# Channel heads of a four-layer kernel: scores and transposed scores issued in bursts of four row groups at both ends of the pipeline

## The reference

```python
# _L3_xattn_ref(q, k, v, gamma), called with (_layernorm(x), ctx, ctx, gamma); h = 8, dq = dv = 16
qh = q.reshape(B, h, dq, Lq)
kh = k.reshape(B, h, dq, Lk)
vh = v.reshape(B, h, dv, Lk)
qk = jnp.einsum('bhdq,bhdl->bhql', qh, kh) * scale
sm = jax.nn.softmax(qk, axis=-1)
ret = jnp.einsum('bhql,bhdl->bhdq', sm, vh)
return gamma * ret.reshape(B, Dv, Lq)
```

## Time and profile before

| | |
|---|---|
| median of 3 runs | 1308.56 us (1308.42 to 1309.82) |
| profiled execution | 1305.17 us, of which the span is 1303.0 us |
| PE busy | 1089.4 us (84%), mean granted clock 0.918 |
| DVE, ACT, POOL busy | 766.5, 494.2, 577.3 us |
| channel heads | about 861 to 1091 us of the span |
| their lead-in (scores alone) | about 873.7 to 887 us |
| their tail (keys alone) | from about 1045 us |
| mixture behind them | from 1091.6 us, its routed tiles from 1130.5 us |

### The profile page before, as it was taken

How to read it: one execution, slowest core, us unless ns; L and a number is a source line. 1 busy time by engine, 2 the same in 40 slices (tenths; PEclk the granted TensorE clock), 3 DMA queues, 4 the chain that set the end, 5 groups by cost and what they waited for, 6 DMA issues and landing times. The chain is left out here.

```text
span 1303.0 us, 25544 instructions
## 1 busy us (share of the span) xinstructions
PE 1089.4 (84%) x7222; PEld 799.5 (61%) x7223; DVE 766.5 (59%) x2814; ACT 494.2 (38%) x1309; POOL 577.3 (44%) x910
## 2 busy tenths in 40 slices
PE   4568799999999983999997999958887795799970
PEld 4355688877777761566655766634554554688860
DVE  6767443244444444687754655457888846555547
ACT  0046221223333320566563234414665532244430
POOL 5550027713333343555561524444333566455550
PEclk9998699999999995899998999977998966899995
DMA  9788962213333327111010234340000622366648
GB/s 399 212 259 280 340 218 108 107 57 110 106 106 106 106 86 314 50 52 64 2 38 22 98 87 134 122 157 1 2 2 2 242 82 84 114 164 164 164 120 320
DMA packets 92301, 169.45 MB, mean 130 GB/s; under 512 B 11102, under 2 KB 70750, under 8 KB 91230
## 3 DMA queue, kind: packets, MB, share of 16 engines
q1 hardware_dynamic: 72393, 107.63, 27.1%
q0 software_dynamic: 17664, 48.91, 10.4%
q10 hardware_dynamic: 2160, 11.86, 2.2%
HBM read 82.75 MB, written 85.61 MB: 129 GB/s over the span
## 5 line engine op out<-in xcount | busy, mean ns | idle before, releaser
L2177 PE MATMUL bank<-weights,xT 128*128 x832 | 240.8, 412 | 0.2 <-ACT xT L2271 0.2
L1999 POOL DMA_INDIRECT slots_out<-weights,y_rows x128 | 122.8, 959 | 134.8 <-DVE y_rows L2443 89.6
L2177 PEld LDWEIGHTS bank<-weights,xT 128*128 128x128 f32 x832 | 142.5, 191 | 24.6 <-issue 0.7
L1993 POOL DMA_INDIRECT slots_in<-xn_wide,row_in x106 | 102.4, 966 | 101.3 <-DMA slots_in<-xs_wide 49.8
L1999 POOL DMA_INDIRECT slots_out<-pack,y_rows x80 | 76.7, 959 | 142.8 <-DVE y_rows L2443 135.3
L2271 ACT COPY xT<-bank 128x256 f32<-128x256 f32 x208 | 77.4, 372 | 116.9 <-PE bank L2169 116.5
L1412 PE MATMUL bank<-ctx,weights 32*128 32x256 f32 x512 | 79.6, 451 | 33.0 <-DVE weights L1566 26.9
L2088 PE MATMUL bank<-xT,weights 128*128 128x256 f32 x416 | 104.5, 396 | 2.3 <-ACT xT L2235 2.3
L1485 ACT ACTIVATE weights<-bank 128x512 f32<-128x512 f32 x128 | 72.6, 596 | 72.0 <-PE bank L1420 72.0
L2420 DVE TENSOR_TENSOR weights<-weights,bank 128x128 f32<-128x128 f32 x128 | 36.8, 288 | 102.4 <-ACT weights L2275 102.4
L1566 DVE TENSOR_REDUCE weights<-bank 128x2 f32<-128x512 f32 x128 | 85.6, 681 | 10.3 <-PE bank L1412 9.8
(11 more groups left out here) (428 smaller groups left out, 2456.4 us busy)
## 6 DMA issues: line engine op xcount, KB each, us to landing
slots_in<-xs_wide SPq DMA_DIRECT2D x16, 2112.0 KB, 19.0
weights<-slots_in SPq DMA_DIRECT2D x96, 132.0 KB, 2.3
xs_wide<-slots_in SPq DMA_DIRECT2D x72, 132.0 KB, 2.3
weights<-slots_out SPq DMA_DIRECT2D x17, 512.0 KB, 11.5
rows<-slots_out SPq DMA_DIRECT2D x16, 512.0 KB, 3.3
weights<-in_l_gu SPq DMA_DIRECT2D x1, 7040.0 KB
pack<-slots_in SPq DMA_DIRECT2D x40, 132.0 KB, 2.1
weights<-in_l_gu ACTq DMA_DIRECT2D x1, 4608.0 KB, 14.4
```

The source lines that it names most:

```text
L1993: pool.indirect_dma_start(out=slots_in, in_=xn_wide[:, t, :], in_offset=None, out_offset=bass.IndirectOffsetOnAxis(ap=row_in[:, t, i:i + 1 ...
L1999: pool.indirect_dma_start(out=slots_out, in_=y[:, n % U, :], in_offset=None, out_offset=bass.IndirectOffsetOnAxis(ap=y_rows[:, n % U:n % U ...
L2177: last = nc.tensor.matmul(out, xT[:, n.c % 2, c, :], flat(gu_w[:, ds(e, 1), c, :]), start=(c == 0), stop=(c == C - 1 and layer != 2))
```

## The change

Scores and keys are no longer always issued two at a time.

- Lead-in: scores 0 to 3, 4 to 7 and 8 to 11 go out in bursts of four, at t = -14, -10 and -6; t = -12, -8 and -4 issue none. From t = -2 on it is as before.
- Tail: keys 116 to 119, 120 to 123 and 124 to 127 go out in bursts of four at t = 116, 120 and 124; t = 118, 122 and 126 issue none. These twelve keys rotate over the six banks 0 to 5 instead of three (`key_bank`); `key_owner` gives the item whose exponential must be done before. Key 116 also waits for all peaks.
- The waits for `b_added` before the lead-in's bursts are for 4, 6 and 8 at t = -14, -10, -6.
- Step 15 issues 24 scatters instead of 28, and the mixture 12 late ones instead of 8.

```diff
-            scatter_in = {13: 6, 14: 6, 15: 28}
+            scatter_in = {13: 6, 14: 6, 15: 24}
...
+            LAST_FOURS = N * NB - 12
+
             def score_bank(s):
                 return bank[s % LEAD] if s < AHEAD else S[s % SB]
+
+            def key_bank(k):
+                return ST[k % TB] if k < LAST_FOURS else bank[k % LEAD]
+
+            def key_owner(k):
+
+                if k < LAST_FOURS:
+                    return k - TB
+                if k - LEAD >= LAST_FOURS:
+                    return k - LEAD
+                return max(m for m in range(LAST_FOURS) if m % TB == k % TB) if k % LEAD >= SB else None
+
+            def scores_at(t):
+                first = t + AHEAD
+                if t < -2:
+                    return range(first, first + 4) if first % 4 == 0 else ()
+                return range(first, min(first + 2, N * NB))
+
+            def keys_at(t):
+                if t >= LAST_FOURS:
+                    return range(t, min(t + 4, N * NB)) if t % 4 == 0 else ()
+                return range(max(t, 0), max(t + 2, 0))
...
-                    queries = [divmod(s, N) for s in (t + AHEAD, t + AHEAD + 1) if s < N * NB]
-                    keys = [divmod(k, N) for k in (t, t + 1) if 0 <= k < N * NB]
+                    queries = [divmod(s, N) for s in scores_at(t)]
+                    keys = [divmod(k, N) for k in keys_at(t)]
...
-                        if N * b + n >= TB:
-                            pe.wait_ge(e_ready, N * b + n - TB + 1)
+                        if N * b + n == LAST_FOURS:
+                            pe.wait_ge(m_ready, N * NB)
+                        owner = key_owner(N * b + n)
+                        if owner is not None and owner >= 0:
+                            pe.wait_ge(e_ready, owner + 1)
...
-                            last = nc.tensor.matmul(ST[(N * b + n) % TB][:, j * L:(j + 1) * L],
+                            last = nc.tensor.matmul(key_bank(N * b + n)[:, j * L:(j + 1) * L],
...
-                    if t < 8 - AHEAD:
-                        pe.wait_ge(b_added, t + AHEAD + 2)
+                    if t in (-14, -10, -6):
+                        pe.wait_ge(b_added, {-14: 4, -10: 6, -6: 8}[t])
...
-                        nc.scalar.activation(eT[:, n].rearrange("p j q -> p (j q)"), ST[t % TB][:], ACT.Exp,
+                        nc.scalar.activation(eT[:, n].rearrange("p j q -> p (j q)"), key_bank(t)[:], ACT.Exp,
...
-            mixture(3, rt, carve, LAST, scattered, 8)
+            mixture(3, rt, carve, LAST, scattered, 12)
```

## The result

| | before | after |
|---|---|---|
| median | 1308.49 us (1307.88 to 1309.82, 4 runs) | 1295.93 us (1294.64 to 1296.95, 4 runs) |
| ratio of the medians | | 0.9902, 95% interval 0.9885 to 0.9919 |
| profiled execution | 1305.17 us, span 1303.0 | 1296.95 us, span 1294.9 |
| the same pair again, in a later series | 1308.15 us (11 runs) | 1297.07 us (6 runs), ratio 0.9914 (0.9899 to 0.9930) |

The kernel is 12.6 us faster in the first series and 11.1 us in the later one; 1299.7 was forecast, that is 8.9 us.

The account below looks back on a forecast made before the run. The prediction took POOL's scatters, held up by the channel heads' tail on half-clock PE, as the bound. Tail -10.4, block's end +0.5 and lead-in +1.0 gave -8.9 us: 1308.56 to 1299.7 us, range 1296.3 to 1305.0.

Parts of the forecast that it names:

- The clock in the tail: Channel heads' tail: PE's granted clock rises from half to full 3 to 5.5 us after t = 116 starts.
- rival A: Tail: the clock stays at one half to the end, gain only 3.0 us, 1305.6 us; chance 0.15.
- Rival C: Tail: bursts of four don't run abreast, each takes 4 us, tail gains 0, 1310.1 us; chance 0.03.
- rival B: Lead-in: bursts with gaps keep the clock low in the batches behind; slower, 1310.5 us; chance 0.04.
- PE's chain and ACT's behind it: Tail: at full clock ACT's row sets values(15,1), starting 12.4 us after t = 116 instead of 23.57.
- The cap: POOL's first sixteen scatters of step 15 let at most 10.9 us of the tail's gain through; 10.4 taken.
- The block's end, +0.5: POOL's ninth scatter after the hole now waits for the block's end: 0.5 us cost, bounds 0 and 1.0.
- The lead-in, +1.0: Lead-in: two DVE stalls of 0.7 us, partly absorbed, plus 0.2 for the clock: +1.0 us, bounds 0 and 2.3.
- the sum, -10.4 + 0.5 + 1.0 = -8.9: Whole kernel: tail, block's end and lead-in terms added, giving a median of 1299.7 us; chance 0.67.
- case D: Lead-in and block's end cost nothing: 1298.2 us, or 1297.7 with the full cap; chance 0.11.
- The profiled execution: Whole kernel's profiled time: 1305.17 - 8.9 = 1296.3 us, its 3.4 us under the median carried over.

Follow-up runs that it names:

- the last experiment: Tail's fours, lead-in in pairs, two scatters moved to step 12, with 22 scatters in step 15 and 12 late instead of 26 and 8: 1298.39 us, 0.9929.
- the lead-in alone: Kernel before with only the lead-in's bursts of four; tail in pairs, 28 scatters in step 15, 8 late: 1308.28 us, ratio 1.0002.
- before, 2nd: Kernel before, unchanged, run and profiled again in a later series: 1307.58 us, ratio 0.9992.
- all four kernels: On the slower chip, against before (1438.29 us): before again 1438.74, tail alone 1434.15, lead-in alone 1436.52, before with filler products 1439.02 us.
- The tail's part: Kernel before with only the tail's bursts of four; lead-in in pairs, 28 scatters in step 15, 8 late: 1296.66 us, ratio 0.9910.

## Why the prediction was right, and where it was off

**The clock in the tail, right.** The full clock was expected 3 to 5.5 us behind the start of t = 116 and came after 2.65 us, a little sooner than that. The row of transposes right behind the first burst did no harm. The rule cited from the Trainium skill (TensorE: Matmul & The Clock Gate, Part 4: PE-mode transpose) would have made this rival A, 1305.6 us; the rows of after refute that outcome here. They don't show what a transpose counts for by itself. Rival C is out by the first burst of sixteen records, 2.09 us where it wanted 4, and rival B by the lead-in's clock, which rose sooner and not later (below).

**PE's chain and ACT's behind it, right within 1 us.** The last values were forecast 12.4 us after t = 116 and came after 11.5.

**The cap, right, and taken too low.** The prediction set 10.9 us as the most that POOL's sixteen scatters let through, and took 10.4. The slots came 1.4 us before the seventeenth scatter began, so the cap was reached in full: from the start of t = 116 to the last scatter it is 76.1 us before and 65.15 after, 10.9 us less. 0.5 us mis-sized.

**The block's end, +0.5, measured 0.** The step named DVE's entry into the mixture as the bound for the ninth scatter. The bound exists (1.1 us in the last experiment), but it moved with the tail: once the hole had closed, the block's work was done before POOL got there. The ninth scatter started 11.5 us behind the last slot instruction (1082.60 less 1071.09), DVE's entry came after 10.9 (1081.95). The error was to compare the ninth scatter with the block's end, both at their old distance from L1808 (the ninth at 10.39 us behind it, the bound at 10.9). With the cap taken as binding, the same working would have had POOL at its own pace there, and not at L1808's.

**The lead-in, +1.0, measured 0 to 0.3.** The stalls came as drawn, two of 0.64 us, and the first subtraction of peaks 0.92 us later. But it doesn't last: 0.3 us were left at t = 116. What fits this is the granted clock, which rose for the batches behind after 21.3 us from the first score (876.00 to 897.3) instead of 24.85 (873.75 to 898.6), and in the lead-in alone after 21.5. For the clock the prediction had added 0.2 us of loss; by this reading it gave some 0.6 back, and no run separates it from other slack.

**The step that failed: the sum, -10.4 + 0.5 + 1.0 = -8.9.** Its mechanism held, but all three terms were mis-sized to the same side. The largest miss is the lead-in's +1.0, which measured 0 to 0.3; the block's end, +0.5, measured 0; the tail's -10.4 measured -10.9. With the measured sizes the sum is -10.6 to -10.9, and from the first score to the end the traces give 10.4 to 10.9. That is case D with the full cap, which the prediction put at 1297.7; the later series has 1297.07. This accounts for 1.7 to 2.0 us of the miss of 3.8 us (1299.7 to 1295.93).

The rest is no term of the change that a trace shows. It lies between some 10.9 us in the stage and a difference of medians of four runs each, 12.6 us with an interval from 10.6 to 15.0; the later series, with 11.1 us (9.2 to 13.2), agrees with the stage. What part of the first 12.6 is chance can't be said more closely. The prediction's range had no term for it: its lower end lay 1.4 us below case D with the full cap, and the first median 0.4 us below that end.

**The profiled execution: near, by luck.** 1296.3 us was forecast and 1296.95 measured. The change gave more than the sum said, and this execution reached the channel heads 2.25 us later than the one of before (876.00 against 873.75); the two largely cancel. The 3.4 us by which the profiled execution of before lay under its median were carried over as if they belonged to the kernel; the one of after lay 1.0 us above its own median. This didn't move the forecast of the median, which is 1308.56 - 8.9 with or without it, but such offsets are why the two whole profiled executions, 8.2 us apart, don't measure the change.

Most of the 3.4 us can be seen to arise long ahead of the change. The windows of a stretch of low clock in before, and in before, 2nd, whose own time is 1308.6 us, 1.0 above its median:

```profile
130.00:151.00 21.00, 13.98 (x59) 12.50 (x60) 9.32 (x38) 5.27 (x12) 2.55 (x5) 0.51 1.09 341
151.00:158.00 7.00, 6.02 (x35) 5.00 (x34) 3.12 (x18) 1.40 (x4) 0.00 (x0) 1.00 1.09 341
```

```profile
130.00:151.00 21.00, 14.13 (x59) 12.65 (x60) 9.16 (x38) 5.27 (x12) 2.56 (x5) 0.51 1.09 341
151.00:158.00 7.00, 6.54 (x22) 4.98 (x21) 2.10 (x9) 1.14 (x3) 0.00 (x0) 0.53 1.09 341
```

The same kernel got its full clock at 151.0 us in one execution and at 157.6 in the other. With it, PE issued 35 matmul records from 151 to 158 us instead of 22, and the lead-in began at 873.75 instead of 876.88. Followed instruction by instruction, DVE lies 0.25 us later at 152.0 us, 2.6 at 155.2 and 2.9 at 185.5. In the profile of the lead-in alone the clock rose at 151.8 us too, and it lies 3.2 us under its median (1305.12 against 1308.28). Both profiles of after had the late rise (156.7 and 156.6 us) and lie about at their median: 1296.95 against 1295.93, and 1296.92 against 1297.07. So the offset is a matter of the execution and not of the kernel; within one series before ran from 1302.44 to 1310.89 us.

## What to carry to other kernels

When PE is busy all the time at half clock, look at how many row groups its products occupy before looking for work to remove: bursts of two row groups kept PE 97% busy at half speed for 23.9 us, and the same bursts with unread products on the other two row groups brought the full clock and 9.4 us. How soon it comes differs between executions (2.6 to 3.9 us here, once 7.4). Where a chain is shortened behind a queue that issues at a fixed pace, the queue's own row is the gain's limit, and terms counted behind it must be measured from the queue, not from the chain. And a change is sized between two rows of the trace that enclose it, and not by the length of two profiled executions: here 7 us of clock, 700 us ahead of the change, moved one of them by 3 us.

## What the runs showed of the hardware

- Filler on idle row groups cost no time here: keys and filler 0.02 us apart, 0.79 and 0.80 us each at half clock, 0.38 and 0.38 at the full one.
- One chip ran all four kernels 130 us (10%) longer than the others, with a mean granted clock of 0.88 to 0.89 against 0.91 to 0.93. In the tail PE, ACT and DVE stood for up to 12 us, much of it together, while POOL worked on. The tail's part, 11.3 us on the other chip, gave 4.1 there (ratio 0.9977, interval 0.9960 to 0.9994).
- Executions of one kernel differ by up to 8.45 us on one chip (1302.44 to 1310.89). Two profiles of it differ by 2.9 us behind one stretch in which the clock rose 6.6 us sooner in one of them.
- Indirect scatters issued in a row start 1.27 us apart in every profile (0.96 us each, 0.30 between).
